# A prologue with twice-normalised tokens, a bias from TensorE and a gate folded into the projection

## The chip, the cores and the metric

The kernel runs on one core of a Trainium2 chip. The metric is the device time of one execution in microseconds; the shown time is the median of three runs.

## The reference

The input x has 2048 tokens of 128 features. One layer of attention and one of experts follow, each wrapped in two norms. The part that matters here is how q, k and v are made:

```python
y = layernorm(x)                                     # plain, eps 1e-5
x_norm = layernorm(y) * ln_w + ln_b                  # the second norm, with weights
q = l2norm(split_heads(x_norm @ Wq))                 # 16 heads of 8 features
k = l2norm(split_heads(x_norm @ Wk))
v = split_heads(y @ Wv)                              # from y, not from x_norm
resonance = sigmoid((q . k - THRESH) * SHARP)        # no softmax
gate_q, gate_k = q . gq, k . gk                      # one number per head and token
out = (resonance * gate_q * gate_k) @ v, then @ Wo + bo
```

The attention output goes through a layernorm and is added to x; then come a router, eight experts of which two are taken per token, a shared expert, a last layernorm and a second addition.

## The kernel before, in words

Tokens are handled in four blocks of 512 (`NB`, `TB`), each of four tiles of 128 tokens (`SUB`). The kernel is written by hand with semaphores: each engine has its own program, its queue is run in order, and a `wait_ge` holds everything behind it.

**The prologue** makes for each block q and k (transposed, each as a high and a low half-precision part, repeated in four slots) and the values times their key gate. `PROLOGUE` (line 83) is the order in which ScalarE and TensorE go through it; VectorE has its own order (lines 1114 to 1125). A block goes through these steps:
- `tokens`: VectorE writes (x - mean) * rstd of the first norm into `tok` (L1050). TensorE turns the four tiles into the bank UB (`turn_hidden`, L716), and ScalarE copies it to `hT` (L595).
- `project`: TensorE multiplies each tile of `hT` with `w_qkv` (384 columns in single precision, L730), with the banks GB and OB in turn. Tile j waits until tile j - 2 has been copied out (L729). ScalarE copies each bank to `raw` (L604).
- `unit` (VectorE): four operations (L1083) scale q and k by `fac2`, which turns the first norm into the second, add the bias row `b_qk` and write `qk`; `gk_prod` and `gk_s` (L1090, L1091) are k . gk; ScalarE squares `qk` (`square`, L608); then the sum over heads (L1095), a reciprocal root of nine small operations, and the scaling of `qk` in place (L1101), which lets `unit_ready` rise. In blocks 1 and 2 `tokens` of the next block stands within it.
- `gated_values` (L1104) writes `vg`. `high_parts` (ScalarE, L614) copies `qk` to half precision, `low_parts` (VectorE, L1112) writes the rest, GpSimd repeats both in free slots (L538): high q, high k, low q, low k.
- `turn`: TensorE transposes q and k (L749, four groups of eight), ScalarE copies them out (L624); for the last block VectorE does (L1130). TensorE's `turn_hidden` of the next block waits for all four copies (`qk_copied`).

Between these steps stand single "rounds" of block 0's attention: four score products (L769), two sigmoids of 1024 columns on ScalarE (L658), and eight value products (L783, one round later). There are 64 rounds per block of queries; eight of block 0 stand in the prologue. After it round follows round, and in the second to fourth block the experts' work lies between rounds.

**Set-up.** The bias row is one product of the broadcast `ln_b` (`lnb_all`) with the weights before they are scaled (L707); `set_up` (L1053) copies it to `b_qk` and scales the q and k weights by `ln_w` in place. `set_up` stands on VectorE between `tokens(0)` and the norms of the other twelve tiles. Loads are issued at the start on SyncE and ScalarE; SyncE also stores q of each block and later reads it back.

Of the kernel before, what the change touches and what calls it, by code (L numbers as in the profile page):

```python
# [34 lines left out]
F = 512  # L35
FC = F // P
NT = 15
NU = NT + 1
# [69 lines left out]
def build(nc, x, wqkv, vecs, consts, ident16, wo, router, gu, down, out):  # L108
    ctx = ExitStack()
    with ctx:  # L110
# [91 lines left out]
        with ExitStack() as pro_ctx:  # L202
            def scratch(name, shape, dt=F32):
                return pro_ctx.enter_context(nc.sbuf_tensor(name, shape, dt))

            x_sb = scratch("x_sb", [P, ST, D])
            w_qkv = scratch("w_qkv", [P, 3 * D])
            lnb_all = scratch("lnb_all", [P, P])
            b_qk = scratch("b_qk", [P, 2 * D])
# [3 lines left out]
            gk_prod = scratch("gk_prod", [P, SUB * H, HD])  # L213
# [4 lines left out]
        raw = [m.rearrange("p (s n) -> p s n", s=SUB)  # L218
               for m in (pwork[:, TB:4 * TB], coll[:, 0:3, :].rearrange("p g t -> p (g t)"))]

        q_out = y_tok[:].rearrange("p n s d -> p (n s d)").bitcast(F16).rearrange("p (g t) -> p g t", g=NG)
        qk = pwork[:, 4 * TB:6 * TB].rearrange("p (w n) -> p w n", w=2)
        sq = pwork[:, 6 * TB:8 * TB].rearrange("p (n d) -> p n d", d=HD)
# [53 lines left out]
        setup = sem("setup")  # L277
        bias_mm = sem("bias_mm")
        pro = sem("pro")
# [4 lines left out]
        raw_ready = sem("raw_ready")  # L284
        qk_ready = sem("qk_ready")
        sq_ready = sem("sq_ready")
# [297 lines left out]
        def _(act):  # L584
# [12 lines left out]
            def project(b):  # L597

                if b >= 2:

                    act.wait_ge(vg_ready, b - 1)
                for j in range(SUB):
                    act.wait_ge(qkv_mm, b * SUB + j + 1)
                    nc.scalar.activation(raw[b % 2][:, j, :], (GB, OB)[j % 2][:, 0:3 * D], ACT.Copy).then_inc(raw_ready, 1)  # L604

            def square(b):
                act.wait_ge(qk_ready, b * SUB + SUB)
                nc.scalar.activation(sq, qk.rearrange("p w n -> p (w n)").rearrange("p (n d) -> p n d", d=HD),  # L608
                                     ACT.Square).then_inc(sq_ready, 1)

            def high_parts(b):
                act.wait_ge(unit_ready, b + 1)
                for w in (0, 1):
                    nc.scalar.activation(split[:, w, :, 0, :], qk[:, w, :].rearrange("p (n d) -> p n d", d=HD),  # L614
                                         ACT.Copy).then_inc(hi_ready, 1)

# [84 lines left out]
        def _(pe):  # L701

            pe.wait_ge(setup, 3)
# [15 lines left out]
            def project_qkv(b, turned):  # L719

                pe.wait_ge(hT_ready, b + 1)
                if b == 0:

                    pe.wait_ge(setup, 5)
# [62 lines left out]
            def gate_rows(i, g, before):  # L787

                pe.wait_ge(*before)
                if i == 0 and g == 0:  # L790

                    pe.wait_ge(setup, 8)
                nc.tensor.matmul(GB[:], gm_a[:], qT[:, g, :], start=True, stop=False)  # L793
                nc.tensor.matmul(GB[:], gm_b[:], qT[:, g, :], start=False, stop=True).then_inc(gateb_mm, 1)  # L794
# [202 lines left out]
        def _(dve):  # L997
# [34 lines left out]
            def norms(j0, j1):  # L1032
# [8 lines left out]

                link(v.tensor_tensor(fac2[:, j0:j1], fac12[:, 0, j0:j1], var12[:, 0, j0:j1], ALU.mult))
                link(v.tensor_tensor(fac2[:, j0:j1], fac2[:, j0:j1], fac12[:, 1, j0:j1], ALU.mult))

            def tokens(b):


                wait(dve, hT_mm, b)
                for j in range(b * SUB, (b + 1) * SUB):
                    v.tensor_scalar(tok[:, j % SUB, :], x_sb[:, j, :], mv[:, j, 0:1], fac12[:, 0, j:j + 1],  # L1050
                                    ALU.subtract, ALU.mult).then_inc(h_ready, 1)

            def set_up():  # L1053

                dve.wait_ge(bias_mm, 1)
                v.tensor_copy(b_qk[:], GB[:, 0:2 * D]).then_inc(setup, 1)
                v.tensor_scalar(w_qkv[:, 0:2 * D], w_qkv[:, 0:2 * D], col(V_LNW), None, ALU.mult).then_inc(setup, 1)

            def gate_weights():

                v.tensor_copy(gq16[:, 0:1], col(V_GQ)).then_inc(setup, 1)
                dve.wait_ge(setup, 6)
                link(v.tensor_tensor(gq_parts[:, 0:1], col(V_GQ), gq16[:, 0:1], ALU.subtract))
# [8 lines left out]

            unit_k = qk[:, 1, :].rearrange("p (n d) -> p n d", d=HD)
            unit_q = qk[:, 0, :].rearrange("p (n d) -> p n d", d=HD)

            def unit(b):


                wait(dve, hi_ready, b * 2)
                wait(dve, lo_ready, b * 2)  # L1080
                for j in range(SUB):
                    dve.wait_ge(raw_ready, b * SUB + j + 1)
                    v.scalar_tensor_tensor(  # L1083
                        out=qk[:, :, j * D:(j + 1) * D], in0=raw[b % 2][:, j, 0:2 * D].rearrange("p (w n) -> p w n", w=2),
                        scalar=fac2[:, b * SUB + j:b * SUB + j + 1], in1=b_qk[:].rearrange("p (w n) -> p w n", w=2),
                        op0=ALU.mult, op1=ALU.add).then_inc(qk_ready, 1)
                dve.wait_ge(qk_ready, b * SUB + SUB)

                gk = vec_sb[:, V_GK:V_GK + HD].unsqueeze(1).to_broadcast([P, SUB * H, HD])
# [10 lines left out]
                both = qk.rearrange("p w n -> p (w n)").rearrange("p (n d) -> p n d", d=HD)  # L1100
                v.tensor_tensor(both, both, rn_t[:].unsqueeze(2).to_broadcast([P, NQK, HD]), ALU.mult).then_inc(unit_ready, 1)  # L1101

            def gated_values(b):
                v.tensor_tensor(vg[:, b * SUB:(b + 1) * SUB, :, :],  # L1104
                                raw[b % 2][:, :, 2 * D:3 * D].rearrange("p s (h d) -> p s h d", d=HD),
                                gk_s[:].rearrange("p (s h) -> p s h", s=SUB).unsqueeze(3).to_broadcast([P, SUB, H, HD]),
                                ALU.mult).then_inc(vg_ready, 1)

            def low_parts(b):
                for w, of in ((0, unit_q), (1, unit_k)):  # L1110
                    dve.wait_ge(hi_ready, b * 2 + w + 1)
                    v.tensor_tensor(split[:, w, :, LOW_SLOT[w], :], of, split[:, w, :, 0, :], ALU.subtract).then_inc(lo_ready, 1)  # L1112

# [336 lines left out]
def _layout(inputs):  # L1450
# [25 lines left out]
        "x": a["attn_x"].reshape(ST, P, D).transpose(1, 0, 2),  # L1476
        "wqkv": np.concatenate([a["attn_Wq"], a["attn_Wk"], a["attn_Wv"]], axis=1),
        "vecs": vecs, "consts": consts, "ident16": half,
# [21 lines left out]
```

## Time and profile before

| | before |
|---|---|
| median of three runs | 769.53 us (768.27 to 771.33) |
| the profiled execution | 772.57 us, of which the span is 770.8 us |
| TensorE busy in the span | 636.3 us (83%) |
| ScalarE | 569.5 us (74%) |
| VectorE | 431.0 us (56%) |
| GpSimd | 161.8 us (21%) |
| mean granted TensorE clock | 0.923 |

The page takes one execution apart. The span runs from the first to the last instruction; 1.8 us lie around it. PE is TensorE's products, PEld its weight loads, DVE VectorE, ACT ScalarE, POOL GpSimd, SP SyncE. A busy share is a mean over stages with different limits, so the stage around the change is read on its own. The granted clock is 1.00 at 2.4 GHz and 0.50 at 1.2 GHz. A single-precision product is recorded as two matmul records.

### The profile page before, as it was taken

The numbers are of one execution on the slowest core, as the hardware profiler recorded it, in microseconds if no ns is written. First come the engines' busy times: TensorE is split into PE (matmuls) and PEld (weight loads), VectorE is DVE, ScalarE is ACT, GpSimd is POOL, SyncE is SP. The second block draws the span as 40 slices with busy tenths as digits, with TensorE's granted clock in tenths as the row PEclk, the third lists the DMA queues.
The fourth block names the chain that finished last, engine by engine and source line by source line (L and its number), as shares of the span: only waits on it lengthen the run. The fifth ranks groups of instructions, "written<-read, shape, count | busy, mean of one in ns | idle before, by whom it ended". The sixth has DMA issues, their size and how long they took to land.

```text
span 770.8 us, 15214 instructions
## 1 busy us (share of the span) xinstructions
PE 636.3 (83%) x5866; PEld 252.6 (33%) x5866; DVE 431.0 (56%) x1126; ACT 569.5 (74%) x661; POOL 161.8 (21%) x149
## 2 busy tenths in 40 slices
PE   4478999999899999998599999987799999327850
PEld 2232211113213444432034444421234444116740
DVE  6997277702624555546525455376245464685963
ACT  2479899997998888879598888797688888003520
POOL 1122000000041122230412112314011211342432
PEclk9778999999999999999799999998899999757985
DMA  9500002600054444120624443103434530137931
GB/s 331 191 28 29 35 5 95 246 22 8 1 159 137 134 139 151 42 59 1 191 76 143 130 135 94 52 12 110 120 113 132 152 120 20 39 107 248 294 116 37
DMA packets 47639, 82.02 MB, mean 106 GB/s; under 512 B 5456, under 2 KB 25168, under 8 KB 47568
## 3 DMA queue, kind: packets, MB, share of 16 engines
q1 hardware_dynamic: 45088, 76.31, 30.4%
q0 software_dynamic: 2048, 4.20, 1.8%
q8 instruction: 47, 0.77, 0.4%
q10 hardware_dynamic: 432, 0.54, 0.3%
q14 instruction: 24, 0.20, 0.1%
HBM read 64.58 MB, written 16.45 MB: 105 GB/s over the span
## 4 chain that ended last, share of the span: by engine, by line
PE 57%; ACT 18%; DVE 12%; issue 4%; DMA 3%; POOL 2%; SPq 1%; POOLq 0%; DVEq 0%
PE AV L783 25%; ACT res L658 15%; PE S L769 11%; PE UO L857 9%; PE GB L857 5%; DMA gu_ring<-gu_dram 2%; DVE work L1245 2%; PE UO L806 1%; DVE work L1378 1%; ACT work L632 1%; POOL xs_dram L551 1%; POOL y_tok L564 1%; DVE coll L1139 1%; PE GB L793 1%; DVE pwork L1083 1%
## 5 line engine op out<-in xcount | busy, mean ns | idle before, releaser
L658 ACT ACTIVATE res<-S 128x1024 f32<-128x1024 f32 x478 | 463.7, 1045 | 74.3 <-PE S L769 72.1
L783 PE MATMUL AV<-res,vg 128*8 128x512 f32 x2048 | 300.4, 612 | 15.9 <-DVE coll L1139 15.9
L769 PE MATMUL S<-qT,kT 32*128 32x512 f16 x956 | 144.3, 393 | 19.6 <-ACT res L658 14.9
L579 POOL TENSOR_TENSOR work<-work 128x512 f32<-128x512 f32 x64 | 82.0, 1282 | 293.0 <-DVE work L1252 292.9
L769 PEld LDWEIGHTS S<-qT,kT 32*128 32x128 f16 x956 | 37.3, 91 | 254.1 <-ACT res L658 201.1
L551 POOL DMA_INDIRECT xs_dram<-xrow,slot x32 | 31.6, 989 | 215.2 <-DVE slot L1232 206.7
L632 ACT ACTIVATE work<-work,scl 128x512 f32<-128x512 f32 x64 | 46.2, 722 | 40.1 <-DVE work L1245 39.9
L1245 DVE TENSOR_SCALAR work<-GB,scl 128x512 f32<-128x512 f32 x56 | 45.3, 809 | 50.1 <-PE GB L857 50.0
L1252 DVE SCALAR_TENSOR_TENSOR work<-work,scl,UO 128x512 f32<-128x512 f32 x56 | 41.7, 744 | 40.7 <-PE UO L857 40.3
L783 PEld LDWEIGHTS AV<-res,vg 128*8 128x8 f32 x2048 | 34.2, 87 | 79.8 <-issue 27.7
L1396 DVE TENSOR_SCALAR gate_q<-GB 128x512 f32<-128x512 f32 x16 | 11.1, 692 | 80.7 <-PE GB L794 80.7
L1264 DVE TENSOR_TENSOR hid_lo<-work,hid_hi 128x512 f16<-128x512 f32 x64 | 53.9, 841 | 3.2 <-ACT hid_hi L648 1.6
L1272 DVE COPY xT<-UO 128x256 f16<-128x256 f16 x45 | 12.8, 290 | 70.3 <-PE UO L852 70.3
L857 PE MATMUL GB<-xT,gu_ring 128*128 128x128 f16 x624 | 44.0, 220 | 5.6 <-DMA gu_ring<-gu_dram 2.5
L857 PE MATMUL UO<-xT,gu_ring 128*128 128x128 f16 x624 | 43.7, 220 | 2.7 <-DVE work L1278 2.7
L857 PE MATMUL UO<-dn_ring,hid_hi 128*128 128x128 f16 x424 | 42.2, 222 | 2.8 <-DVE hid_lo L1264 2.8
L857 PEld LDWEIGHTS GB<-xT,gu_ring 128*128 128x128 f16 x624 | 35.7, 98 | 15.3 <-issue 12.0
L658 ACT ACTIVATE res<-UO 128x1024 f32<-128x1024 f32 x34 | 39.7, 1166 | 0.2 <-PE S L769 0.2
L857 PEld LDWEIGHTS UO<-xT,gu_ring 128*128 128x128 f16 x624 | 35.5, 98 | 11.7 <-issue 11.7
L857 PE MATMUL UO<-dn_ring,hid_lo 128*128 128x128 f16 x212 | 38.8, 221 | 0.0
L564 POOL DMA_INDIRECT y_tok<-ys_dram,slot x32 | 30.5, 953 | 33.8 <-DMA ys_dram<-work 25.2
L857 PEld LDWEIGHTS UO<-dn_ring,hid_hi 128*128 128x128 f16 x424 | 31.1, 98 | 12.7 <-issue 9.5
(210 smaller groups left out, 610.8 us busy)
## 6 DMA issues: line engine op xcount, KB each, us to landing
gu_ring<-gu_dram SPq DMA_DIRECT2D x60, 512.0 KB, 3.6
dn_ring<-dn_dram SPq DMA_DIRECT2D x60, 256.0 KB, 3.4
work<-in_gu SPq DMA_DIRECT2D x8, 512.0 KB, 10.3
gu_dram<-gu_ring SPq DMA_DIRECT2D x8, 512.0 KB, 2.7
ys_dram<-work SPq DMA_DIRECT2D x60, 64.0 KB, 2.6
work<-in_down SPq DMA_DIRECT2D x8, 256.0 KB, 10.8
dn_dram<-dn_ring SPq DMA_DIRECT2D x8, 256.0 KB, 2.9
work<-xs_dram SPq DMA_DIRECT2D x4, 448.0 KB, 4.8
```

The source lines that it names most:

```text
L551: nc.gpsimd.indirect_dma_start(xs_dram, bass.IndirectOffsetOnAxis(ap=slot[:, i % 2, n * SUB + j:n * SUB + j + 1], axis=0), xrow[:, j, :], ...
L564: nc.gpsimd.indirect_dma_start(y_tok[:, n, j, :], None, ys_dram, bass.IndirectOffsetOnAxis(ap=slot[:, i % 2, n * SUB + j:n * SUB + j + 1], ...
L579: nc.gpsimd.tensor_tensor(hid[u % 2], prod[u % 2], sg[u % 2], ALU.mult).then_inc(hid_ready, 1)
L632: nc.scalar.activation(sg[c % 2], gate_c[c % 2], ACT.Sigmoid, scale=scale(S_SIG)).then_inc(sg_ready, 1)
L658: nc.scalar.activation(res[:, k % 2, 2 * half:2 * half + 2, :].rearrange("p h t -> p (h t)"), score_banks(i, k, half).rearrange("p h t -> ...
L769: mm = nc.tensor.matmul(banks[:, j % 2, :], kT[r, g, s * P:(s + 1) * P], qT[r, g, :], start=True, stop=True)
L783: mm = nc.tensor.matmul(AV[32 * j:32 * j + HD, :], vg[:, s, G * g + j, :], res[:, k % 2, j, :], start=s == 0, stop=s == ST - 1)
L857: mm = nc.tensor.matmul(bank, w, v, start=first and n == 0, stop=last and n == 2)
L1245: v.tensor_scalar(gate_c[u % 2], gate_bank(i, u), scale(S_HI), scale(S_LO), ALU.min, ALU.max).then_inc(gate_clipped, 1)
L1252: v.scalar_tensor_tensor(out=prod[u % 2], in0=gate_c[u % 2], scalar=scale(S_PROD), in1=up_bank(i, u), op0=ALU.mult, op1=ALU.mult).then_inc ...
L1264: v.tensor_tensor(hid_lo[:, u % LAG], hid[u % 2], hid_hi[:, u % LAG], ALU.subtract).then_inc(hid_split, 1)
L1272: v.tensor_copy(xT[:, t % 3, :], tile_bank(i, t)).then_inc(tile_turned, 1)
```

## The change

Tokens are written with the factor of both norms at once, so q and k come out of the projection finished but for the bias, and v and the new gate columns come out too large by the second norm's factor, which `fac2` (now its inverse) takes back in the gate. The bias is added by TensorE: in each tile's bank a product of `lnb_all` with the unscaled q, k and gate weights comes first, and `hT` with the scaled ones is added to it. The key gate is 16 more columns of the projection (`Wk` summed with `gk` per head). `raw` holds 400 columns per tile; q and k are squared, normalised, and split where they lie in it, and `qk` and `b_qk` are gone.

```diff
-PROLOGUE = [("tokens", 0), ("project", 0), ("tokens", 1), ("square", 0), ("project", 1), ("high", 0),
+PROLOGUE = [("tokens", 0), ("project", 0), ("square", 0), ("tokens", 1), ("project", 1), ("high", 0),
 ...
 # ScalarE
-                    act.wait_ge(vg_ready, b - 1)
+                    act.wait_ge(lo_ready, 2 * b - 2)
 ...
-                    nc.scalar.activation(raw[b % 2][:, j, :], (GB, OB)[j % 2][:, 0:3 * D], ACT.Copy).then_inc(raw_ready, 1)
+                    nc.scalar.activation(raw[b % 2][:, j, :], (GB, OB)[j % 2][:, 0:NQKV], ACT.Copy).then_inc(raw_ready, 1)
             def square(b):
-                act.wait_ge(qk_ready, b * SUB + SUB)
-                nc.scalar.activation(sq, qk..., ACT.Square).then_inc(sq_ready, 1)
+                act.wait_ge(raw_ready, b * SUB + SUB)
+                nc.scalar.activation(sq..., heads[b % 2], ACT.Square).then_inc(sq_ready, 1)
 # TensorE
-            nc.tensor.matmul(GB[:, 0:2 * D], lnb_all[:], w_qkv[:, 0:2 * D], start=True, stop=True).then_inc(bias_mm, 1)
 ...
-                    nc.tensor.matmul((GB, OB)[j % 2][:, 0:3 * D], hT[:, j * P:(j + 1) * P], w_qkv[:],
-                                     start=True, stop=True).then_inc(qkv_mm, 1)
+                    bank, h, n = (GB, OB)[j % 2], hT[:, j * P:(j + 1) * P], 2 * D + H
+                    nc.tensor.matmul(bank[:, 0:n], lnb_all[:], w_qkv[:, 0:n], start=True, stop=False)
+                    nc.tensor.matmul(bank[:, 0:n], h, w_scaled[:], start=False, stop=True)
+                    nc.tensor.matmul(bank[:, n:NQKV], h, w_qkv[:, n:NQKV], start=True, stop=True).then_inc(qkv_mm, 1)
 # VectorE
-                    v.tensor_scalar(tok[:, j % SUB, :], x_sb[:, j, :], mv[:, j, 0:1], fac12[:, 0, j:j + 1],
+                    v.tensor_scalar(tok[:, j % SUB, :], x_sb[:, j, :], mv[:, j, 0:1], fac12[:, 1, j:j + 1],
 ...
             def set_up():
-                dve.wait_ge(bias_mm, 1)
-                v.tensor_copy(b_qk[:], GB[:, 0:2 * D]).then_inc(setup, 1)
-                v.tensor_scalar(w_qkv[:, 0:2 * D], w_qkv[:, 0:2 * D], col(V_LNW), None, ALU.mult).then_inc(setup, 1)
+                dve.wait_ge(in_qkv, 16)
+                gk = vec_sb[:, V_GK:V_GK + HD].unsqueeze(1).to_broadcast([P, H, HD])
+                link(v.tensor_tensor(gk_prod[:], w_qkv[:, D:2 * D].rearrange("p (h d) -> p h d", d=HD), gk, ALU.mult))
+                link(v.tensor_reduce(w_qkv[:, 2 * D:2 * D + H], gk_prod[:], AX_X, ALU.add))
+                v.tensor_scalar(w_scaled[:], w_qkv[:, 0:2 * D + H], col(V_LNW), None, ALU.mult).then_inc(setup, 1)
 ...
             def unit(b):
-                for j in range(SUB):
-                    dve.wait_ge(raw_ready, b * SUB + j + 1)
-                    v.scalar_tensor_tensor(out=qk..., in0=raw..., scalar=fac2..., in1=b_qk..., ...).then_inc(qk_ready, 1)
-                dve.wait_ge(qk_ready, b * SUB + SUB)
-                link(v.tensor_tensor(gk_prod[:], unit_k, gk, ALU.mult))
-                link(v.tensor_reduce(gk_s[:], gk_prod[:], AX_X, ALU.add))
                 if 0 < b < NB - 1:
                     tokens(b + 1)
                 dve.wait_ge(sq_ready, b + 1)
 ...
-                link.count(v.tensor_tensor(gk_s[:], gk_s[:], rn[:, NQK // 2:NQK], ALU.mult))
                 link(v.tensor_scalar(rn_t[:], rn[:], QK_SCALE, None, ALU.mult))
-                v.tensor_tensor(both, both, rn_t..., ALU.mult).then_inc(unit_ready, 1)
+                v.tensor_tensor(heads[b % 2], heads[b % 2], rn_t..., ALU.mult).then_inc(unit_ready, 1)
+                link(v.tensor_tensor(gk_heads, raw[b % 2][:, :, 2 * D:2 * D + H], rn_heads[:, :, H:2 * H], ALU.mult))
+                link(v.tensor_tensor(gk_heads, gk_heads, fac2..., ALU.mult))
```

`high_parts`, `low_parts` and `gated_values` read the same elements from `raw` instead of `qk`; the weights come with 16 columns of zeros between k and v.

## Rows read from the trace of the kernel before

**Rows 1.** Busy time by stretch; PE, PEld, DVE, ACT, POOL, then granted clock

```profile
12.00:31.00 19.00, 9.26 (x20) 4.20 (x20) 17.77 (x64) 7.06 (x13) 2.79 (x3) 0.93 0.87 321
31.00:45.00 14.00, 9.72 (x49) 5.91 (x50) 13.04 (x28) 10.09 (x14) 3.89 (x6) 0.61 0.09 37
45.00:60.00 15.00, 11.34 (x77) 5.35 (x78) 14.02 (x30) 11.62 (x16) 4.21 (x5) 0.77 0.09 36
60.00:79.00 19.00, 14.67 (x121) 4.57 (x119) 13.34 (x31) 15.63 (x18) 3.30 (x4) 0.82 0.07 29
100.00:125.00 25.00, 25.00 (x168) 4.21 (x164) 15.02 (x36) 24.85 (x29) 0.00 (x0) 1.00 0.07 11
```

**Rows 2.** Chain of waits in the prologue: start, length, what

```profile
29.96 2.55 DVE pwork L1083 x4
...
33.59 0.92 ACT qT L624
...
37.73 1.10 PE UO L716 x4
...
41.23 0.64 ACT pwork L614
...
43.70 2.55 DVE pwork L1083 x4
...
46.27 1.06 ACT pwork L608
...
51.47 1.09 PE UO L716 x4
...
54.93 1.15 PE GB L730 x2
...
58.80 1.38 ACT res L658 x2
...
79.44 1.93 ACT res L658 x2
```

**Rows 3.** Timeline of VectorE in block 1: start, length, operation

```profile
32.53 0.69 DVE L1090 TENSOR_TENSOR gk_prod<-pwork,vec_sb 128x512 f32<-128x512 f32 x1
33.26 0.69 DVE L1091 TENSOR_REDUCE gk_s<-gk_prod 128x64 f32<-128x512 f32 x1
35.01 1.21 DVE L1095 TENSOR_REDUCE ssq<-pwork 128x128 f32<-128x1024 f32 x1
39.33 0.23 DVE L1098 TENSOR_TENSOR gk_s<-gk_s,rn 128x64 f32<-128x64 f32 x1
39.73 1.22 DVE L1101 TENSOR_TENSOR pwork<-pwork,rn_t 128x1024 f32<-128x1024 f32 x1
```

**Rows 4.** Timeline of TensorE: projections, one weight load, and narrow products

```profile
15.26 1.49 PE L730 MATMUL GB<-w_qkv,pwork 128*128 128x384 f32 x2
15.26 0.34 PEld L730 LDWEIGHTS GB<-w_qkv,pwork 128*128 128x128 f32 x1 [0.21 <-issue]
16.54 1.49 PE L730 MATMUL UO<-w_qkv,pwork 128*128 128x384 f32 x2
22.31 0.81 PE L730 MATMUL UO<-w_qkv,pwork 128*128 128x384 f32 x2
181.61 2.94 PE L806 MATMUL UO<-wo_sb,coll 128*128 128x128 f32 x24
```

**Rows 5.** Timeline of ScalarE's copies and GpSimd's repeats

```profile
21.04 0.47 ACT L604 ACTIVATE coll<-GB 128x384 f32<-128x384 f32 x1
38.86 0.60 ACT L595 ACTIVATE pwork<-UO 128x512 f32<-128x512 f32 x1 [1.22 <-PE UO L716]
28.21 3.62 POOL L538 TENSOR_SCALAR pwork<-pwork 128x512 f16<-128x512 f16 x4 [24.17 <-ACT pwork L614]
```

**Rows 6.** Short stretches in which the granted clock rose, columns as in group 1

```profile
41.00:43.00 2.00, 1.40 (x4) 0.48 (x3) 1.66 (x3) 2.00 (x5) 1.06 (x1) 0.79 0.00 0
55.00:57.00 2.00, 2.00 (x5) 1.03 (x6) 1.66 (x3) 1.85 (x5) 1.33 (x2) 0.87 0.00 0
```

More of the change, by code:

```diff
@@ L36 @@
 FC = F // P
+NQKV = 3 * D + H
 NT = 15
@@ L206, in build @@
             x_sb = scratch("x_sb", [P, ST, D])
-            w_qkv = scratch("w_qkv", [P, 3 * D])
+            w_qkv = scratch("w_qkv", [P, NQKV])
+            w_scaled = scratch("w_scaled", [P, 2 * D + H])
             lnb_all = scratch("lnb_all", [P, P])
-            b_qk = scratch("b_qk", [P, 2 * D])
             ssq = scratch("ssq", [P, NQK])
@@ L212, in build @@
             rn_t = scratch("rn_t", [P, NQK])
-            gk_prod = scratch("gk_prod", [P, SUB * H, HD])
+            gk_prod = scratch("gk_prod", [P, H, HD])
             gk_s = scratch("gk_s", [P, SUB * H])
@@ L218, in build @@
         raw = [m.rearrange("p (s n) -> p s n", s=SUB)
-               for m in (pwork[:, TB:4 * TB], coll[:, 0:3, :].rearrange("p g t -> p (g t)"))]
+               for m in (pwork[:, TB:TB + SUB * NQKV], coll[:].rearrange("p g t -> p (g t)")[:, 0:SUB * NQKV])]
+        heads = [m[:, :, 0:2 * D].rearrange("p s (n d) -> p s n d", d=HD) for m in raw]
         q_out = y_tok[:].rearrange("p n s d -> p (n s d)").bitcast(F16).rearrange("p (g t) -> p g t", g=NG)
-        qk = pwork[:, 4 * TB:6 * TB].rearrange("p (w n) -> p w n", w=2)
         sq = pwork[:, 6 * TB:8 * TB].rearrange("p (n d) -> p n d", d=HD)
@@ L599, in project @@
                 if b >= 2:
-                    act.wait_ge(vg_ready, b - 1)
+                    act.wait_ge(lo_ready, 2 * b - 2)
                 for j in range(SUB):
                     act.wait_ge(qkv_mm, b * SUB + j + 1)
-                    nc.scalar.activation(raw[b % 2][:, j, :], (GB, OB)[j % 2][:, 0:3 * D], ACT.Copy).then_inc(raw_ready, 1)
+                    nc.scalar.activation(raw[b % 2][:, j, :], (GB, OB)[j % 2][:, 0:NQKV], ACT.Copy).then_inc(raw_ready, 1)
             def square(b):
-                act.wait_ge(qk_ready, b * SUB + SUB)
-                nc.scalar.activation(sq, qk.rearrange("p w n -> p (w n)").rearrange("p (n d) -> p n d", d=HD),
-                                     ACT.Square).then_inc(sq_ready, 1)
+                act.wait_ge(raw_ready, b * SUB + SUB)
+                nc.scalar.activation(sq.rearrange("p (s n) d -> p s n d", s=SUB), heads[b % 2], ACT.Square).then_inc(sq_ready, 1)
             def high_parts(b):
@@ L613, in high_parts @@
                 for w in (0, 1):
-                    nc.scalar.activation(split[:, w, :, 0, :], qk[:, w, :].rearrange("p (n d) -> p n d", d=HD),
-                                         ACT.Copy).then_inc(hi_ready, 1)
+                    nc.scalar.activation(split[:, w, :, 0, :].rearrange("p (s h) d -> p s h d", s=SUB),
+                                         heads[b % 2][:, :, w * H:(w + 1) * H, :], ACT.Copy).then_inc(hi_ready, 1)
             def turn(b):
@@ L722, in project_qkv @@
                 if b == 0:
-                    pe.wait_ge(setup, 5)
+                    pe.wait_ge(setup, 4)
                 wait(pe, qk_copied, 4 * turned)
@@ L790, in gate_rows @@
                 if i == 0 and g == 0:
-                    pe.wait_ge(setup, 8)
+                    pe.wait_ge(setup, 7)
                 nc.tensor.matmul(GB[:], gm_a[:], qT[:, g, :], start=True, stop=False)
@@ L1040, in norms @@
                     v.tensor_copy(lnb_all[:], col(V_LNB).to_broadcast([P, P])).then_inc(setup, 1)
-                link(v.tensor_tensor(fac2[:, j0:j1], fac12[:, 0, j0:j1], var12[:, 0, j0:j1], ALU.mult))
-                link(v.tensor_tensor(fac2[:, j0:j1], fac2[:, j0:j1], fac12[:, 1, j0:j1], ALU.mult))
+                link(v.tensor_tensor(fac2[:, j0:j1], fac12[:, 1, j0:j1], var12[:, 1, j0:j1], ALU.mult))
+                link(v.tensor_tensor(fac2[:, j0:j1], fac2[:, j0:j1], fac12[:, 0, j0:j1], ALU.mult))
             def tokens(b):
@@ L1097, in unit @@
                 rsqrt(link, ssq[:], rn[:], rn_t[:])
-                link.count(v.tensor_tensor(gk_s[:], gk_s[:], rn[:, NQK // 2:NQK], ALU.mult))
+                rn_heads = rn[:].rearrange("p (s n) -> p s n", s=SUB)
+                gk_heads = gk_s[:].rearrange("p (s h) -> p s h", s=SUB)
                 link(v.tensor_scalar(rn_t[:], rn[:], QK_SCALE, None, ALU.mult))
-                both = qk.rearrange("p w n -> p (w n)").rearrange("p (n d) -> p n d", d=HD)
-                v.tensor_tensor(both, both, rn_t[:].unsqueeze(2).to_broadcast([P, NQK, HD]), ALU.mult).then_inc(unit_ready, 1)
+                v.tensor_tensor(heads[b % 2], heads[b % 2], rn_t[:].rearrange("p (s n) -> p s n", s=SUB).unsqueeze(3)
+                                .to_broadcast([P, SUB, 2 * H, HD]), ALU.mult).then_inc(unit_ready, 1)
+                link(v.tensor_tensor(gk_heads, raw[b % 2][:, :, 2 * D:2 * D + H], rn_heads[:, :, H:2 * H], ALU.mult))
+                link(v.tensor_tensor(gk_heads, gk_heads, fac2[:, b * SUB:(b + 1) * SUB].unsqueeze(2).to_broadcast([P, SUB, H]), ALU.mult))
             def gated_values(b):
                 v.tensor_tensor(vg[:, b * SUB:(b + 1) * SUB, :, :],
-                                raw[b % 2][:, :, 2 * D:3 * D].rearrange("p s (h d) -> p s h d", d=HD),
+                                raw[b % 2][:, :, 2 * D + H:NQKV].rearrange("p s (h d) -> p s h d", d=HD),
                                 gk_s[:].rearrange("p (s h) -> p s h", s=SUB).unsqueeze(3).to_broadcast([P, SUB, H, HD]),
@@ L1109, in low_parts @@
             def low_parts(b):
-                for w, of in ((0, unit_q), (1, unit_k)):
+                for w in (0, 1):
                     dve.wait_ge(hi_ready, b * 2 + w + 1)
-                    v.tensor_tensor(split[:, w, :, LOW_SLOT[w], :], of, split[:, w, :, 0, :], ALU.subtract).then_inc(lo_ready, 1)
+                    hi, lo = (split[:, w, :, n, :].rearrange("p (s h) d -> p s h d", s=SUB) for n in (0, LOW_SLOT[w]))
+                    v.tensor_tensor(lo, heads[b % 2][:, :, w * H:(w + 1) * H, :], hi, ALU.subtract).then_inc(lo_ready, 1)
             dve.wait_ge(in_x, 16)
@@ L1476, in _layout @@
         "x": a["attn_x"].reshape(ST, P, D).transpose(1, 0, 2),
-        "wqkv": np.concatenate([a["attn_Wq"], a["attn_Wk"], a["attn_Wv"]], axis=1),
+        "wqkv": np.concatenate([a["attn_Wq"], a["attn_Wk"], np.zeros((D, H), f), a["attn_Wv"]], axis=1),
         "vecs": vecs, "consts": consts, "ident16": half,
```

14 lines of the change are left out of this document (1 added, 13 removed).

## The prediction

> **What bounds the kernel now.** I read the busy time by stretch first. Up to 31 us VectorE works 17.8 of 19 us, then 13.0 of 14 and 14.0 of 15; from 60 to 79 us ScalarE leads with 15.6 of 19, and after 100 us ScalarE and TensorE are both full, a round each 1.83 us [rows 1]. So only the time up to about 79 us can change, and what follows is moved as a whole by as much as round 8 of the attention starts earlier or later: its first sigmoid stands at 79.44 in the chain of waits [rows 2]. Then I read that chain between 30 and 80 us. It doesn't stay on VectorE: the four scale-and-bias operations (29.96, 43.70), the square (46.27), ScalarE's copies of the turned q and k (33.59), TensorE's turning of tokens (37.73, 51.47), the high parts (41.23), the last projection (54.93) and from 58.80 the sigmoids [rows 2]. VectorE's share is high, but it is one link of a ring in which ScalarE's and TensorE's order of work counts as much.
>
> **Prices.** A projected tile of 384 columns costs TensorE 1.28 us (15.26 to 16.54). The spacing is that of the 1.2 GHz level, whatever the clock column of that stretch says (0.93); at 2.4 GHz I take half, 0.64, to which the 0.81 of two overlapping records at 22.31 fits [rows 1, 4]. After the change a tile has 272 + 272 + 128 = 672 columns in three products: 672/384 = 1.75 times as much, 2.24 us slow, 1.15 fast (the 128 columns at two records of 0.12, from 24 records in 2.94 [rows 4]). A block of four tiles goes from 5.1 to 9.0 us slow, and from 2.6 to 4.6 fast. ScalarE's copy of a tile stays at about 0.5: 0.47 for 384 columns and 0.60 for 512 give 0.01 more for 400 [rows 5].
>
> One price has no row of its own: a weight load ahead of a narrow product at the slow level. The load is recorded at 0.34 there, behind which a record of 0.21 would wait, and 24 loads go unseen within 2.94 us at the fast level [rows 4]. Ends: 0 and 2 x (0.34 - 0.21) = 0.26 us a slow tile, 0.7 us over the 2.6 slow tiles counted below. I take 0, since the spacing of 1.28 us hides the same 0.34. The Trainium skill (TensorE: Matmul & The Clock Gate, LDWEIGHTS) gives a load as its columns over 1.2 GHz, 0.107 us for 128, an estimate by which the load hides and the sum stays; the row shows 0.34, so trace and page differ, and which of the two stands behind a narrow product no row tells.
>
> VectorE loses in each block the four operations (2.55 us) and the two of the key gate (0.69 + 0.69) [rows 2, 3], and gets one more of 64 elements, 0.23 as the one at 39.33, both behind the operation that raises `unit_ready`. From the sum over heads to that point a block keeps 39.73 + 1.22 - 35.01 = 5.9 us [rows 3]. Strided reads instead of contiguous ones: I count 0. At worst the in-place scaling doubles (+1.2 a block), which is hidden below in blocks 1 and 2 (ScalarE reaches the high parts 2 us after VectorE) and in block 3 (it does two rounds first). `set_up` is three short operations for two, about 0.3 us more ahead of the norms, hidden by the projection of block 0, which is late anyway. Without that cover it costs its 0.3. The DMAs keep their number and order; one grows by 16 columns in 384.
>
> **The walk, in the profiled execution's times.** (a) Block 0. GpSimd's repeats start at 28.21, released by the high part [rows 5]; back over 0.65 for that copy and 5.9 for the block's tail, the sum over heads began at 21.6, behind the norms, the next tokens and the four operations. After, it waits for the projection instead: tile 0 starts at 12.7 (15.26 less two tiles), four tiles at the slow level end at 21.7; if the level rises at 18, as it must have somewhere between 17 and 22 [rows 4], at 20.0. Copy and square follow (1.6): 21.6 or 23.3. I take 0 change; the ends are -1.0 (rise at 15) and +1.7.
>
> (b) The first transposes of q and k wait for GpSimd's third repeat, 28.21 + 3 x 0.905 = 30.9, and end at 31.9. Before, ScalarE was then squaring block 1 and copied from 33.59 on [rows 2]; now it squared at 28.6, right behind the high parts, and copies at 32.0: 1.6 earlier, and so are the turned tokens (36.1 for 37.73), the first round and the high parts of block 1 (39.6 for 41.23) [rows 2]. If the tokens that now stand beside the repeats on VectorE slow these, 0.6 less.
>
> (c) Projection of block 2. Tiles 0 and 1 can be made ahead, from 37.9 (36.1, four slow transposes of 1.1 and the copy of 0.6 [rows 2, 5]). At the slow level until 41.9 (the clock rose at 41.8, by 0.79 over 41 to 43 [rows 6]) 1.8 tiles are done, the other 2.2 take 2.5 us: 44.5, copied out at 45.2. Before, TensorE made two tiles in the cover of the high parts, and the last copy ended at 44.9. So 0.3 late: 1.9 us lost here.
>
> (d) But the square then waited for the four operations until 46.27 [rows 2]; now it starts at 45.2, 1.05 earlier. The copies of block 1 and the turned tokens follow: 50.3 for 51.47, and the projection of block 3 starts at 53.7 for 54.9, 1.2 earlier.
>
> (e) It is on the path whole, since TensorE starts it after a round. Slow until 55.5 (0.87 over 55 to 57 [rows 6]): 0.8 tiles; then 3.2 x 1.15 = 3.7: 59.2, with the copy 59.7, where round 2's sigmoids stood at 58.80 [rows 2]. 2.1 us lost; balance +0.9. From there ScalarE's order is the same to 79.44.
>
> The rises of the clock need not keep their times. Before, each came while the projection of that block ran [rows 2, 6]. If it follows that work, which begins 1.6 earlier, (c) ends at 43.7 and (e) at 57.6, and the balance is -0.7. I take the middle, +0.1. The profiled execution of 772.57 becomes 772.7. It lies 3.0 over the median, 769.53, and the same +0.1 on the median gives 769.6.
>
> **Rivals.**
> 1. *The heavier projection keeps TensorE at 2.4 GHz.* For: it is unbroken for 4.6 us and more. Against: between projections there are 5 us of turning, as between 31 and 41 us, where the clock was low (0.61 in the mean [rows 1]). Then (b) ends 0.6 earlier, (c) at 42.6, copied at 43.1, the next projection runs 50.0 to 54.6, its copies end at 55.1 to 55.7: 3.1 early. One more us comes where the sigmoids wait for slow value products (0.82 in 60 to 79 [rows 1]): -4.3, 765.2. The Trainium skill (TensorE: Matmul & The Clock Gate, Part 1) says that the low level is the default and activity lifts it; by that more work at a time would favour this rival. The trace agrees that work lifts it [rows 6].
> 2. *The bias product is paid at 1.2 GHz in both late projections.* For: block 0's tiles were slow for over 5 us [rows 4], and the two rises lie within projections [rows 6]. Then (c) takes 37.9 to 47.0, copied at 47.5; (d) puts the next projection at 56.4, and (e) ends at 65.4, 65.9 with the copy: +7.1, 776.6. It decides once the slow part of the two together is some 6 us longer than in (c) and (e), where it could be 12: each such us costs half of one on top of the +0.9, and +3.9 is the bound below.
> 3. *The added columns are covered.* If TensorE's products were hidden behind the copies and rounds, (b) and (d) stay and (c) and (e) go: -1.6 - 1.2 = -2.8, 766.7. Against: in (e) nothing stands beside the last tiles.
> 4. *VectorE was the path after all*, and every us taken from it counts: 4.0 - 0.2 a block over blocks 1 to 3, -11, 758. Against: ScalarE is busy 44 of 67 us in these stretches [rows 1], and its order puts rounds between the parts.
>
> **How the numbers follow.** Forecast 0.63 (769.6, own range 767 to 772.5), rival 1 0.15, rival 2 0.14, rival 3 0.06, rival 4 0.02. About 0.5%, 3.9 us, is what a measurement of this kernel can tell from no change. Faster: three quarters of rival 1, rival 4 and a little of the forecast's tail, 0.17. Slower: nearly all of rival 2 and as little of the tail, 0.17. Same: 0.66. The range leaves out the outer parts of rivals 1 and 2: 765.0 to 774.5.
>
> **What would show it.** Projections of four tiles that take 5 to 9 us where they took 2.6 to 5.1; VectorE idle ahead of the sum over heads, released by ScalarE's square; the square of block 1 right behind the high parts of block 0; round 2's sigmoid within 1.5 us of 58.80 and round 8's of 79.44. It is wrong if round 8 starts ahead of 76 or after 83 us, if the clock's level in the late projections differs from the half-and-half of the walk, or if the time after round 8 changes, which I hold fixed.

## The result and the profile after

| | before | after |
|---|---|---|
| median of 20 runs | 769.62 us (767.77 to 771.33) | 766.73 us (765.42 to 770.08) |
| the profiled execution, its span | 772.57, 770.8 us | 766.72, 764.9 us |
| TensorE, its weight loads | 636.3, 252.6 us | 634.9, 262.0 us |
| VectorE, ScalarE | 431.0, 569.5 us | 420.4, 569.1 us |
| mean granted clock | 0.923 | 0.939 |

The medians lie 2.9 us apart; the ratio of the two kernels is 0.9972 (95%: 0.996 to 0.9983), which is 2.2 us (1.3 to 3.1). Four of after's 20 times lie at 769.9 to 770.1, which draws the ratio towards 1. The change is smaller than the half per cent that the prediction had called no change, but its median is 2.9 us from the 769.6.

First, where the 5.9 us between the two spans lie. VectorE computes the query gate once in 16 rounds; the two times of a row are the first and the last such operation. The row of before, and then that of after:

```profile
L1396 DVE TENSOR_SCALAR gate_q<-GB x16: 690/692/692, 94.1 to 658.6; 128x512 f32<-128x512 f32 x16
```

```profile
L1382 DVE TENSOR_SCALAR gate_q<-GB x16: 690/692/693, 91.4 to 654.0; 128x512 f32<-128x512 f32 x16
```

The prologue with its first rounds gives 2.7 us, the stretch between the gates 1.9 (562.6 for 564.5), the tail 1.3 (110.9 for 112.2). The last two are mostly not the change's: before's profiled execution lay 3.0 us over its median, and two kernels below that are built on before show 563.7 and 563.8 for that stretch, and 110.9 and 110.7 for the tail. Over all kernels below the stretch has 562.6 to 564.9, and with it goes the time that TensorE spends at 1.2 GHz there (see the fillers). The prologue's 2.7 is near the 2.9 between the medians; since only this one execution of before was profiled, how much a typical one loses there is not shown.

After's busy time by stretch (columns as in [rows 1]), and two short stretches:

```profile
12.00:31.00 19.00, 12.33 (x56) 10.06 (x56) 15.70 (x61) 8.24 (x14) 3.21 (x4) 0.99 0.88 324
31.00:45.00 14.00, 11.75 (x70) 9.10 (x69) 10.88 (x25) 9.63 (x14) 3.56 (x5) 0.65 0.10 39
45.00:60.00 15.00, 11.23 (x98) 7.34 (x95) 8.22 (x19) 12.53 (x18) 3.31 (x4) 1.00 0.09 36
60.00:79.00 19.00, 14.93 (x124) 5.12 (x124) 13.02 (x31) 16.24 (x19) 3.31 (x4) 0.91 0.15 57
40.00:42.00 2.00, 2.00 (x11) 1.73 (x10) 1.73 (x3) 1.30 (x4) 1.68 (x2) 0.82 0.00 0
60.00:62.00 2.00, 0.93 (x10) 0.72 (x11) 1.86 (x5) 1.91 (x3) 0.00 (x0) 0.80 0.00 0
```

VectorE's time falls as foretold: 8.2 of 15 us from 45 to 60, where it was 14.0. The number to look at is the clock: 1.00 from 45 to 60 for 0.77, and 0.91 from 60 to 79 for 0.82 [rows 1]. The clock rises at about 40.7, holds until about 61.2, and is low again until about 64.6; before it was low from about 48.7 to 55.5 and from about 69.2 to 76.0.

The chain of waits of after, answering to [rows 2] (start, length, what):

```profile
31.86 1.03 ACT qT L622
...
36.12 1.10 PE UO L711 x4
...
37.89 1.27 PE GB L726 x2
...
44.13 0.51 ACT pwork L603
44.67 1.06 ACT pwork L607
45.73 1.84 ACT y_tok L622 x2
...
49.48 0.64 PE UO L711 x4
...
57.14 1.37 ACT res L656 x2
58.85 1.07 ACT pwork L607
...
76.81 1.93 ACT res L656 x2
```

VectorE has left the chain here: the square (44.67, L607) follows the last copy (44.13) at once, where it waited for VectorE until 46.27 [rows 2]. The tokens of block 3 are turned at 49.48 in 0.64 us, where it took 1.09 from 51.47 on. Round 2's sigmoids stand at 57.14 for 58.80, round 8's at 76.81 for 79.44.

VectorE after, answering to [rows 3]:

```profile
21.23 1.22 DVE L1077 TENSOR_REDUCE ssq<-pwork 128x128 f32<-128x1024 f32 x1 [2.29 <-ACT pwork L607]
30.11 1.72 DVE L1047 TENSOR_SCALAR tok<-x_sb,mv,fac 128x128 f32<-128x128 f32 x4
36.33 1.23 DVE L1083 TENSOR_TENSOR coll<-coll,rn_t 128x1024 f32<-128x1024 f32 x1
37.72 0.22 DVE L1086 TENSOR_TENSOR gk_s<-gk_s,fac 128x64 f32<-128x64 f32 x1
41.91 2.05 DVE L1047 TENSOR_SCALAR tok<-x_sb,mv,fac 128x128 f32<-128x128 f32 x4
```

It idles ahead of the sum over heads, released by the square (L607). The strided scaling in place takes 1.23 us for 1.22: strided reads cost nothing, as counted.

TensorE after: tiles of the first projection, the end of the projection of block 2, then the stretch after the second turning:

```profile
12.73 1.27 PE L726 MATMUL GB<-w_qkv,lnb_all 128*128 128x272 f32 x2 [0.69 <-ACT pwork L594]
15.13 1.11 PE L726 MATMUL UO<-w_qkv,lnb_all 128*128 128x272 f32 x2
17.12 0.62 PE L726 MATMUL GB<-w_qkv,lnb_all 128*128 128x272 f32 x2
18.26 0.62 PE L726 MATMUL UO<-w_qkv,lnb_all 128*128 128x272 f32 x2
...
43.71 0.38 PE L728 MATMUL UO<-w_qkv,pwork 128*128 128x128 f32 x2
...
49.48 0.63 PE L711 MATMUL UO<-const_sb,tok 128*128 128x128 f32 x4 [1.18 <-issue]
50.04 0.40 PE L766 MATMUL S<-qT,kT 32*128 32x512 f16 x4
50.37 1.04 PE L780 MATMUL AV<-res,vg 128*8 128x512 f32 x8
51.34 0.73 PE L726 MATMUL GB<-w_qkv,lnb_all 128*128 128x272 f32 x2
54.06 0.72 PE L726 MATMUL GB<-w_qkv,lnb_all 128*128 128x272 f32 x2 [0.17 <-ACT coll L603]
```

A slow tile takes 2.40 us (12.73 to 15.13), a fast one 1.14 (17.12 to 18.26). From 49.48 on all is at the fast level: turning, scores, eight value products in 1.04 and a projection from 51.34 on. From the end of the projection of block 2 (43.71 and 0.38) to the scores of round 1 (50.04) there are 5.9 us. The two rows that answer to these in before, 8.1 us apart:

```profile
43.56 0.81 PE L730 MATMUL UO<-w_qkv,pwork 128*128 128x384 f32 x2
...
52.49 0.61 PE L769 MATMUL S<-qT,kT 32*128 32x512 f16 x4
```

### The profile page after: what moved, and what is told of

Same layout as the page of the kernel before. It is cut to its first block, busy times and chain, and to the rows that moved or that the text cites. A ratio compares the mean times of both kernels' runs of the same rounds, so it can differ in the third digit from the quotient of the medians.

```text
span 764.9 us, 15312 instructions
## 1 busy us (share of the span) xinstructions
PE 634.9 (83%) x5928; PEld 262.0 (34%) x5928; DVE 420.4 (55%) x1107; ACT 569.1 (74%) x661; POOL 161.3 (21%) x149
## 4 chain that ended last, share of the span: by engine, by line
PE 58%; ACT 19%; DVE 13%; issue 5%; POOL 2%; DMA 2%; POOLq 0%; DVEq 0%
PE AV L780 24%; ACT res L656 17%; PE S L766 10%; PE UO L854 9%; PE GB L854 5%; DVE work L1231 2%; PE UO L803 2%; DVE work L1238 1%; DVE work L1364 1%; PE UO L746 1%; ACT work L630 1%; POOL xs_dram L550 1%; POOL y_tok L563 1%; PE GB L726 1%; DVE coll L1125 1%
## 5 line engine op out<-in xcount | busy, mean ns | idle before, releaser
L656 ACT ACTIVATE res<-S 128x1024 f32<-128x1024 f32 x478 | 463.3, 1045 | 71.5 <-PE S L766 69.5
L780 PE MATMUL AV<-res,vg 128*8 128x512 f32 x2048 | 295.2, 601 | 15.9 <-DVE coll L1125 15.9
```

The lines of the kernel that those rows point to most:

```text
L656: nc.scalar.activation(res[:, k % 2, 2 * half:2 * half + 2, :].rearrange("p h t -> p (h t)"), score_banks(i, k, half).rearrange("p h t -> ...
L780: mm = nc.tensor.matmul(AV[32 * j:32 * j + HD, :], vg[:, s, G * g + j, :], res[:, k % 2, j, :], start=s == 0, stop=s == ST - 1)
```

## Experiments

The theories, by the letters that the expectations use. A: the heavier projection itself keeps the clock up. B: the added columns are a price, and nothing else. C: the gain is VectorE's freed time; E says the same, but where fillers are tried it says that the clock is incidental. D: in before, and wherever the square waits for VectorE's four operations, the turning of a block is so long that TensorE drops to 1.2 GHz within it and makes the late projection partly slow; after takes the wait away, the turning shortens, and the clock holds. A to C were stated before the first four experiments, D and E after their results. The labels in brackets are those by which the expectations refer to a kernel. Each kernel was profiled in one execution.

**Without the bias product** (`e1_light`). The edit, on after:

```diff
-                    nc.tensor.matmul(bank[:, 0:n], lnb_all[:], w_qkv[:, 0:n], start=True, stop=False)
-                    nc.tensor.matmul(bank[:, 0:n], h, w_scaled[:], start=False, stop=True)
+                    nc.tensor.matmul(bank[:, 0:n], h, w_scaled[:], start=True, stop=True)
```

> The changed kernel without the bias product in each tile (the bias is left out): 400 projected columns a tile instead of 672. Theory A, the heavier projection keeps TensorE at 2.4 GHz through the turning of block 1 and the projection of block 3, and that is where the gain came from: with less work the clock falls again between 46 and 56 us, and the time is 1 us above the changed kernel's, about 767.8. Theory B, the columns are only a price and the clock is not tied to them: 3 to 4 us below, about 763. Theory C, the gain is VectorE's shorter path and TensorE's work is covered: no change, 766.7 within 0.7.

Measured: 765.24 us, ratio 0.9949 (0.9934 to 0.9964). Its stretch from 45 to 60, and its round 8:

```profile
45.00:60.00 15.00, 10.16 (x92) 5.93 (x96) 9.69 (x25) 13.41 (x19) 3.30 (x4) 0.98 0.15 59
```

```profile
73.38 3.77 ACT L656 ACTIVATE res<-S 128x1024 f32<-128x1024 f32 x4 [2.65 <-PE S L765]
```

With 272 columns a tile fewer the clock is held all the same (0.98), and the kernel is 1.5 us faster, round 8 3.4 earlier, of which 1.1 goes again between the gates (563.7 for 562.6). Theory A falls. The 3 to 4 us of theory B are reached at round 8 and not in the median.

**Before with a heavier projection** (`e2_heavy`). The edit, on before, ahead of each tile:

```diff
+                    nc.tensor.matmul((GB, OB)[j % 2][:, 0:2 * D + H], lnb_all[:], w_qkv[:, 0:2 * D + H], start=True, stop=True)
```

> The kernel before with a product of 272 columns ahead of each projected tile, whose result is overwritten: 656 columns a tile. Theory A: the granted clock stays at 1.00 between 46 and 56 us, and this repays most of the added work: 769.6 to 770. Theory B: the clock falls at about 49 us as before and the work costs 1.3 to 2 us: 771 to 771.6. Theory C: no change, 769.6 within 0.7.

Measured: 772.44 us, ratio 1.0041 (1.0026 to 1.0057).

```profile
45.00:60.00 15.00, 11.41 (x66) 6.53 (x65) 12.49 (x28) 10.30 (x15) 4.04 (x5) 0.77 0.10 36
```

The same columns on before leave the clock at before's 0.77 (it falls at about 50.2) and cost 2.6 us against the 769.84 of before beside it, more than the 1.3 to 2 of theory B. Columns are a price (1.5 us in after, 2.6 in before).

**The old order of the prologue** (`e3_order`). The edit, on after:

```diff
-PROLOGUE = [("tokens", 0), ("project", 0), ("square", 0), ("tokens", 1), ("project", 1), ("high", 0),
+PROLOGUE = [("tokens", 0), ("project", 0), ("tokens", 1), ("square", 0), ("project", 1), ("high", 0),
```

> The changed kernel with the old order on ScalarE, the square of block 0 behind the copy of the next tokens. All theories: the square starts 0.6 us later, and 0.1 to 0.6 us are lost, about 767.0; a loss over 1.5 us would say that the order was a main part of the gain.

Measured: 768.29 us, ratio 0.9977 (0.9963 to 0.999); round 8 at 77.21. By the medians 1.6 us are lost, just over the 1.5 that the expectation had set for a main part of the gain; by round 8 it is 0.4 (77.21 for 76.79), and the interval of the ratio overlaps after's for the most part. So a main part isn't shown, and a part of some tenths of a microsecond isn't excluded.

**VectorE's four operations put back, and waited for** (`e4_stt`). The edit, on after:

```diff
-                act.wait_ge(raw_ready, b * SUB + SUB)
+                act.wait_ge(dq_ready, b * SUB + SUB)
 ...
+                wait(dve, dq_ready, b * SUB)
+                for j in range(SUB):
+                    dve.wait_ge(raw_ready, b * SUB + j + 1)
+                    v.scalar_tensor_tensor(out=dq[:, j, :], in0=raw..., scalar=fac2..., in1=w_scaled...).then_inc(dq_ready, 1)
```

> The changed kernel with the four scale-and-add operations per block put back on VectorE (into a buffer that nobody reads), and the square waiting for them as it did. Theories A and B: VectorE now has slack ahead of the sum over heads in blocks 0 and 3, and 1 to 2.5 us are lost, about 768.5. Theory C: VectorE's path is what was shortened, and putting back the four operations gives back the whole gain or more: 769.6 or above.

Measured: 773.88 us, ratio 1.0061 (1.0045 to 1.0078). Its chain of waits and its stretch from 45 to 60:

```profile
47.03 0.51 ACT pwork L605
47.57 0.50 DVE dq L1079
48.09 1.06 ACT pwork L609
...
53.23 1.09 PE UO L713 x4
...
56.69 1.21 PE GB L728 x2
```

```profile
45.00:60.00 15.00, 11.39 (x73) 7.42 (x72) 11.57 (x26) 10.22 (x15) 3.52 (x5) 0.77 0.09 35
```

The square (48.09) waits for the last such operation, the tokens are turned slowly (1.09 for 0.64), and the projection begins slow (1.21 for 0.73). The clock is back at before's 0.77, and 7.1 us are lost, more than the whole gain; round 8 stands at 82.30, 5.5 later. The expectation of theory C was met and that of A and B missed; what the 7.1 us are made of, the next two experiments take apart.

**The same operations, not waited for** (`e5_stt_free`). The edit, on the kernel just above:

```diff
-                act.wait_ge(dq_ready, b * SUB + SUB)
+                act.wait_ge(raw_ready, b * SUB + SUB)
```

> The four scale-and-add operations per block put back on VectorE as in e4_stt, but the square does not wait for them. Theory D: what the change took away is the square's wait for these operations; it shortens the turning of block 1 on TensorE, so the clock stays at 2.4 GHz until round 1, and e4_stt lost 2.5 us by the wait and 3 us by the fall of the clock that followed. Then VectorE's time alone costs 0.3 us: 767 to 767.5, and the clock does not fall before 58 us. Rival E: VectorE's time itself was the path; then most of the loss of e4_stt stays, 771 to 774.

Measured: 767.07 us, ratio 0.9968 (0.995 to 0.9985). ScalarE with its square and its round 8, and the stretch from 45 to 60:

```profile
45.16 0.50 ACT L605 ACTIVATE pwork<-UO 128x400 f32<-128x400 f32 x1 [0.64 <-PE UO L730]
45.70 1.06 ACT L609 ACTIVATE pwork<-pwork 128x1024 f32<-128x1024 f32 x1
...
77.82 3.77 ACT L658 ACTIVATE res<-S 128x1024 f32<-128x1024 f32 x4 [2.59 <-PE S L768]
```

```profile
45.00:60.00 15.00, 11.66 (x102) 7.66 (x100) 12.37 (x28) 12.33 (x18) 3.63 (x4) 1.00 0.09 35
```

VectorE is nearly as busy as in before (12.4 of 15 us, where it was 14.0; the two operations of the key gate were not put back), and the time is 0.3 us over after's, well inside the intervals. At round 8 the profiled execution is 1.0 later than after's (77.82 for 76.79), so a small price of VectorE's time isn't excluded; the 5.5 at round 8 and 7.1 in the median that the kernel with the wait loses are not it. Theories C and E fall. What counts is the wait: that edit alone takes 773.88 to 767.07, and without the wait the clock holds to about 62.9.

**The wait, with the clock held by filler products** (`e6_stt_fill`). The edit, on the kernel that waits; results of the fillers are not used:

```diff
+FILL_AHEAD, FILL = (8, 0, 0, 0), ((0, 5, 1, 2), (0, 5, 1, 2), (0, 3, 1, 0), (0, 0, 0, 0))
+            def fill(n):
+                for _ in range(n):
+                    nc.tensor.matmul(GB[:, 0:2 * D], lnb_all[:], w_qkv[:, 0:2 * D], start=True, stop=True)
 ...
+                fill(FILL_AHEAD[b])      # ahead of the turning
+                    fill(FILL[b][n])     # behind each turned group
```

> e4_stt, with the four operations and the square's wait, and products of 256 columns into a bank that nobody reads in TensorE's idle time around and between the turnings, so that the clock does not fall. Theory D: 3 to 4 us of e4_stt's loss come back, 769.7 to 771, while the wait stays. Rival E, the clock is incidental: 773.9 within 0.7.

Measured: 770.25 us, ratio 1.0007 (0.9994 to 1.002).

```profile
45.00:60.00 15.00, 13.99 (x104) 9.68 (x103) 13.00 (x28) 11.43 (x16) 3.96 (x5) 1.00 0.09 36
60.00:79.00 19.00, 15.13 (x144) 6.55 (x143) 13.07 (x31) 16.41 (x20) 3.30 (x4) 1.00 0.12 47
```

Of the 7.1 us 3.6 go (773.88 to 770.25) with nothing changed but TensorE's clock and its fillers; the other 3.5 stay with the wait. Round 8 shows the same: 78.47, 3.8 earlier than with the wait and no fillers.

**Before, and after, with the clock held** (`e7_before_fill`, `e8_after_fill`). The same `fill` on before (16 ahead of block 0, the same behind the groups) and on after (8 ahead; other counts behind the groups, 15 in all for 20).

> The kernel before with the same filling products in TensorE's idle time, nothing else. Theory D: the clock holds through the prologue and the late projections run at 2.4 GHz, 1.8 us less, about 768.0. Rival E: 769.8 within 0.7, or more, as each filler can hold up a real product by 0.4 us.

> The changed kernel with filling products. Theory D: the fall at 30.5 us goes, the projection of block 2 runs at 2.4 GHz throughout, and so do the rounds after 61 us: 1.6 us less than the changed kernel, about 765. Rival E: 766.7 within 0.7.

Measured: before with fillers 769.42 us, ratio 0.9994 (0.9981 to 1.0007); after with fillers 766.29, ratio 0.9964 (0.9949 to 0.9979). Both missed theory D's expectation (768.0 and 765), and both lie where rival E, the clock is incidental, had put them (769.8 and 766.7, within 0.7). Before with fillers, around its last low stretch:

```profile
45.00:60.00 15.00, 12.81 (x101) 7.59 (x100) 14.25 (x31) 11.73 (x16) 4.12 (x5) 1.00 0.09 35
71.00:73.00 2.00, 1.68 (x10) 0.22 (x10) 1.79 (x8) 2.00 (x3) 1.30 (x3) 0.63 0.00 0
73.00:75.00 2.00, 2.00 (x16) 0.23 (x12) 0.23 (x2) 0.90 (x2) 0.00 (x0) 0.52 0.00 0
```

After with fillers, its round 8 and its gates:

```profile
74.48 3.77 ACT L657 ACTIVATE res<-S 128x1024 f32<-128x1024 f32 x4 [2.60 <-PE S L774]
```

```profile
L1390 DVE TENSOR_SCALAR gate_q<-GB x16: 690/691/692, 89.1 to 652.9; 128x512 f32<-128x512 f32 x16
```

Holding the clock in before moves round 8 from 79.43 to 78.58 only, and a fall at about 71.5 to 75 us stays: the clock alone is not what before lacked. After with fillers has round 8 at 74.48, 2.3 before after's, but 1.2 us go between the gates (563.8 for 562.6) and 0.3 in the tail (111.2 for 110.9), and its median is 0.4 below after's, less than the intervals tell apart. With fillers in both, the change is worth 4.1 us at round 8 (78.58 to 74.48) and 3.1 in the medians. And with fillers in both, the wait costs 4.0 at round 8 (78.47 for 74.48) and 4.0 in the medians (770.25 for 766.29; the numbers of fillers differ, 20 for 15 behind the groups): that is its price with the clock at 1.00 in both. On the medians alone rival E stands in these two kernels; it falls in the one that waits, where the clock was worth 3.6.

What the 1.2 us between the gates go with can be read from the clock there. In after it does not fall between 200 and 220 us, in after with fillers it does, and around 370 to 390 us it is low for about 10 us where it was 7. The row of after, and then that of after with fillers:

```profile
200.00:220.00 20.00, 17.73 (x142) 4.73 (x140) 11.65 (x42) 17.72 (x22) 6.07 (x7) 1.00 0.27 85
```

```profile
200.00:220.00 20.00, 18.30 (x136) 4.24 (x128) 10.29 (x40) 17.81 (x21) 7.56 (x8) 0.91 0.31 102
```

Over all thirteen profiles the length goes with the time at 1.2 GHz between the gates, summed from the clock column in windows of 10 us. The three with 17 us have 562.6 to 562.8, one with 20 us has 562.9, the seven with 24 us have 563.7 or 563.8, and the two with 27 us (before, and the wait with fillers) have 564.5 and 564.9.

**The bias at half precision** (`e9_narrow`). The lighter projection of the first experiment, with the bias kept: in blocks 1 to 3 one half-precision product in place of two passes, with its high and low part on two halves of the rows. The edit, on after (the lines that make `bias16` and `even16` are not shown):

```diff
-                    nc.tensor.matmul(bank[:, 0:n], lnb_all[:], w_qkv[:, 0:n], start=True, stop=False)
+                    if b == 0:
+                        nc.tensor.matmul(bank[:, 0:n], lnb_all[:], w_qkv[:, 0:n], start=True, stop=False)
+                    else:
+                        nc.tensor.matmul(bank[:, 0:n], even16[:], bias16[:], start=True, stop=False)
```

> The changed kernel with the bias product of blocks 1 to 3 in half precision: the bias row is made once after the projection of block 0, split by VectorE in a high and a low half, and added by one product of 272 columns and one pass. Theory D (columns are a price on the path of the late projections, the clock follows the gaps): between the changed kernel and e1_light, 1 to 1.5 us below the changed kernel, 765.2 to 765.8. Rival E (VectorE's time is the path): the two added operations cost 0.6 us, 767.3.

Measured: 765.68 us, ratio 0.9952 (0.9935 to 0.9969), round 8 at 74.77. This is in theory D's range and 1.6 under rival E's; it lies 1.0 under after's median and 2.0 at round 8, and the intervals of the two ratios overlap a little.

**The same with fillers** (`e10_narrow_fill`; 9 ahead of block 0, behind the groups as in after with fillers).

> e9_narrow with filling products as in e8_after_fill. Theory D: the clock holds to the end of the prologue; round 8 starts at 72 us or before, and the median is 0.5 to 2 us below e9_narrow's, 764 to 765. Rival: what the fillers save in the prologue is given back after round 8, as in e8_after_fill: as e9_narrow within 0.5.

Measured: 762.87 us, ratio 0.9919 (0.9902 to 0.9936), the best of all: 6.7 us under before.

```profile
60.00:79.00 19.00, 15.19 (x132) 4.15 (x124) 10.16 (x24) 16.41 (x20) 3.30 (x4) 1.00 0.11 44
```

```profile
L1407 DVE TENSOR_SCALAR gate_q<-GB x16: 690/692/692, 88.0 to 650.6; 128x512 f32<-128x512 f32 x16
```

The clock is held through the prologue, and the stretch between the gates has the short length (562.6), so that nothing is given back. Round 8 stands at 73.31 for 74.77 without fillers; the 72 that was expected is missed, and the median is 1.1 us under the range. Of the 2.8 us between the medians, 1.5 are gained by round 8 and 1.1 between the gates (562.6 for 563.7).

**After once more** (`e11_after_again`).

> The changed kernel once more, for its clock in another execution. Theory D: where the time is near 766.5, the clock holds from the projection of block 2 to 58 us, and the mean granted clock is 0.938 or more; executions near 770 have 0.934 or less, as when it falls in the turning of block 1. Rival: time and mean clock are not related.

Measured: 766.97 us, ratio 0.9973 (0.9958 to 0.9988); the clock held from about 41 to 61.5, round 8 at 76.69. Time and mean clock go together as theory D has it: nine times from 765.83 to 767.50 have 0.937 to 0.942, three from 769.82 to 770.78 have 0.931 to 0.934. None of these three was profiled, so where the clock fell in them is not shown. Round 8 repeats after's to 0.1 us.

## Why the prediction was wrong

- **What bounds the stage: right.** VectorE's share was high and its time was not the path: the four operations put back without the wait cost 0.3 us in the median (767.07), less than the intervals tell apart. Rival 4, 758, is dead.
- **Prices: right.** Slow tile 2.40 us for 2.24, inside the bound of 0.26 a tile; fast 1.14 for 1.15; copies 0.50. Two sums of the rivals are off by a little: 3.1 and 1 make 4.1 in rival 1, not 4.3, and in rival 2 a copy that ends 2.3 later (47.5 for 45.2) puts the next projection at 56.0, not 56.4. Neither changes on which side of the half per cent its rival lies.
- **Step (a): right.** The repeats start at 27.79 for 28.21, a gain of 0.4 where the count was 0.
- **Step (b): right to 0.2 us.** 31.86, 36.12 and 39.61 against 32.0, 36.1 and 39.6. GpSimd's repeats did not lengthen with the tokens beside them (3.46 and 3.30 us for 3.62).
- **Step (c): right but for the clock.** The projection starts at 37.89 as foretold, and the last copy ends at 44.6 instead of 45.2, since the rise came at about 40.7, not 41.9.
- **Step (d): right in kind.** The square follows the copy (44.67 for 45.2) and the turned tokens come at 49.48 for 50.3.
- **Step (e): the one that failed.** "Slow until 55.5" was taken over from before, where TensorE fell at 48.7 inside the turning of block 1. But (d) had just shortened that turning: from the end of the projection of block 2 to the scores of round 1, with hardly anything but transposes between, TensorE had 8.1 us in before (44.4 to 52.5) and 5.9 in after (44.1 to 50.0), and in after it did not fall. The other kernels agree: 7.3 us in the heavier before and in the variant with the wait, both with the fall; 5.9 again without the bias product, with the old order, with the operations not waited for, with the bias at half precision and in after once more, none with it. So the stretch from turned tokens to projection took 1.86 us (49.48 to 51.34) where 3.4 was forecast, and round 2's sigmoids stand at 57.14 for 59.7: 0.8 us of this from (d), 1.5 from that stretch, 0.2 from the projection. The projection itself gains so little, although all of it is fast, since its third tile (54.06) waits for ScalarE's copies, which stand behind sigmoids and high parts. The prediction's other reading, in which the rises follow the work, ended at 58.1 with the copy; measured, it is 1.0 earlier still, as that reading too kept the slow 3.4 us from turned tokens to projection. Of the prediction's own signs, the level in the late projections differed from its half-and-half, and both marks lie outside its 1.5 us (1.7 and 2.6).
- **"From there ScalarE's order is the same to 79.44": the order was, the time not.** From round 2 to round 8 it took 19.7 us (57.14 to 76.81) for 20.6, with the clock at 0.91 for 0.82. With the 1.7 at round 2 this is the 2.6 of the prologue. The prediction held this stretch fixed; it had named the slow value products between 60 and 79 us as a price in rival 1 alone.

The part on the clock asked only whether its rises follow the work, and never whether its fall would still happen. Rival 1 had the consequence (clock held, late projection fast) and the wrong cause: less work held it as well, and more work in before didn't. The cause shown is the wait that was removed: put back, it costs 7.1 us (6.8 against the same operations without it), 3.6 of them by the clock. The shares of 0.8, 1.5, 0.2 and 1.0 above are read from one execution of each kernel; with fillers in both, where the level differs little, the change is still worth 4.1 us at round 8, so they don't say how much of the gain needs the clock. Rival 3's number, 766.7, was met by luck: its columns are not covered, since without them the kernel is 1.5 us faster.

Three things stay open. The waiting variant of after (773.88) is 1.4 us slower than the heavier before (772.44), of which 1.05 stand at round 8 already (82.30 for 81.25); to this I give no cause. The length of the stretch between the gates goes with the time at 1.2 GHz there and makes up to 2.3 us of one execution, nearly as much as the change; why one execution has a fall of the clock more than another was not found. And the two operations of the key gate that the change took from VectorE were never put back by themselves.

## What to carry to other kernels

Before a stretch is priced at a level of the clock, ask whether the edit changes what puts TensorE there: a wait removed from another engine's queue can shorten TensorE's thin stretch, and then the products behind it can run at twice the clock. An engine that is busy 14 of 15 us need not be the path; what is on the path is the wait on its last instruction, and putting the operations back once with and once without that wait tells the two apart. A change of 0.3% needs a mark inside the kernel, such as the start of round 8, since later stages vary by as much.

## What the runs showed of the hardware

- **A slow tile of three products takes more than its columns.** The slow tile's 2.40 us is 0.16 over the 1.75 times 1.28 that its columns make. By the load that the Trainium skill gives (TensorE: Matmul & The Clock Gate, LDWEIGHTS), 0.107 us for 128 columns, it would by estimate have been hidden whole; the runs don't separate the load from other costs of a third product, so only the 0.16 is shown.
- **The clock column did not show the slow start.** From 12 to 31 us after has 0.99, while its tiles were spaced at 2.40 us until about 17 and at 1.14 behind; the spacing is the better witness there.
- **VectorE's token operations lengthen beside GpSimd's repeats.** Four took 1.72 us at 30.11 and 2.05 at 41.91 while GpSimd repeated the parts (27.79 to 31.25, 40.33 to 43.63), and 1.11 where GpSimd stood idle (47.97, in the kernel with the wait put back). The Trainium skill (SBUF — State Buffer, Who interferes with whom) says that VectorE and GpSimd share a pair of ports, which this kind of operation can ask for; the trace agrees as far as that the four take 1.55 and 1.85 times as long.
